# The sequence of a two-way GRU kept as channel, image, token, and one semaphore in place of two ahead of the candidate scan

## The chip, the cores and the metric

One Trainium2 chip, one of its cores. The metric is the device time of one launch in microseconds. A core has TensorE (matmuls; PE in the profile, PEld for its weight loads), VectorE (DVE), ScalarE (ACT), GpSimd (POOL) and SyncE (SP, whose queue issues the DMAs here). They run side by side and are ordered by semaphores: an instruction may wait until a counter has reached a value, and may raise a counter when it ends. SBUF and PSUM have 128 partitions; "a step" below is the distance between neighbouring elements of one partition.

## The reference

The input x is [16, 32, 32, 128] in f32: 16 images of 32 x 32 tokens of 128 channels.

```
xn   = layernorm(x) * gamma + beta                    # over the channels
gray = mean of xn over the channels                   # [16, 32, 32]
idx  = argmax of a small MLP on gradients of gray     # one choice per image
seq  = xn by rows, or by columns where idx == 1       # [16, 1024, 128]
z    = seq @ in_w.T + in_b
xp   = z @ wih.T + bih                                # per direction, 3 gates
for each of 1024 tokens (one direction forwards, one backwards), for all 16 images:
    gh = h @ whh.T + bhh
    r  = sigmoid(xr + hr);  u = sigmoid(xz + hz)
    n  = tanh(xn_ + r * hn)
    h  = (1 - u) * n + u * h
out  = x + concat(h forwards, h backwards) @ out_w.T + out_b
```

## The kernel before

**First stage, sixteen images.** An image is loaded to `xin` with 8 tokens per partition (image q in slot q mod 4). VectorE takes statistics (L728, L733), ScalarE the square root (`deviation`, L408), VectorE the reciprocal and the shift (`scales`, L740 and L743). ScalarE normalises 2 of the 8 tokens (L414), GpSimd the other 6 (L359). TensorE transposes the image into two PSUM banks, 4 x 128 columns each (L524). ScalarE then copies each bank twice, with gamma and beta (`evacuate`): to `seq` in the order of rows (L426) and to `seq_v`, a view of `big`, in the order of columns (L430); 512 columns per partition each time. VectorE sums the gray values (L754).

Per image, ScalarE's queue is in this order: normalise image q, first half of the writes of image q-1, square root of image q+1, second half of the writes of q-1. VectorE's is: statistics of q+1, gray sums of q-1, reciprocal and shift of q+1. TensorE folds in_w and wih into one weight (L537, L541) between the transposes of images 7 and 8.

**Scores.** After the last image the gray values go through some small matmuls (L552, L561, L565 and on) and some thirty VectorE instructions, one behind the other, to a mask of 16 images. ScalarE's square of the recurrent weights (L460) feeds a matmul (L557) that stands ahead of L561 in TensorE's queue. VectorE then copies `seq_v` over `seq` where the mask is set (`select`, copy_predicated, L856): the first and last 32 tokens at once, the other 960 in sixteen parts during the first sixteen rounds.

**Second stage, 1,024 rounds.** A round makes one step forwards (d = 0) and one backwards (d = 1). Both go through the same chain, half a round apart: TensorE multiplies the state, split in two f16 halves, with the recurrent weights for the reset gate, the candidate and the update gate, three matmuls of 16 columns each (`step`); ScalarE takes the reset gate's sigmoid (L488) and the update gate's (L491); VectorE makes the candidate's argument with a scan (`candidate`, L881); ScalarE takes tanh (L494); VectorE makes the new state (L892) and splits it (L901), and holds u * h ready (L908). Between the two steps of a round TensorE also does a part of the work for the block of 8 tokens that follows: a bias matmul, and one input product (`fill_input`, f32, two matmul instructions of 128 columns: 8 tokens x 16 images of `seq` as the moving operand), or an output projection (L872 adds it to x). All these matmuls are recorded at L590.

The candidate scan waits for two things, the reset gate from ScalarE and the recurrent product from TensorE:

```
dve.wait_ge(reset_ready[d], turn)
dve.wait_ge(hn_ready[d], turn)
```

An instruction carries one wait; of two in a row one becomes an instruction of its own (EVENT_SEMAPHORE, here at L880). TensorE's own order has two waits ahead of a step's reset group as well: the state's halves and `reset_ready` of the other direction.

The layouts: `seq` is [128, 1024 tokens, 16 images], the view `seq_v` the same. The same memory `big` later holds the tiles of x to which the output is added; the tiles of a block lie where tokens of `seq_v` lay that are already selected.

Of the kernel before, what the change touches and what calls it, by code (L numbers as in the profile page):

```python
# [20 lines left out]
P = 128  # L21
B, H, WD, C = 16, 32, 32, 128
L = H * WD
DI = 2 * C
HID = 128
TB = 8
# [74 lines left out]
def build(nc, x, gamma, beta, w1t, b1, w2t, b2, in_w, in_b, wiht, whht, bih, bhh, outwt, out_b, consts, out):  # L101
    ctx = ExitStack()

    def sb(name, shape, dt=F32):
        return ctx.enter_context(nc.sbuf_tensor(name, shape, dt))

    def sem(name):
        return ctx.enter_context(nc.semaphore(name))


    seq = sb("seq", [P, L, B])
    big = sb("big", [P, L * B])
    seq_v = big[:, :].rearrange("c (t b) -> c t b", b=B)
    tiles = big[:, :].rearrange("p (k c) -> p k c", c=C)
    xin = sb("xin", [P, SLOTS, TPP, C])
    stats = sb("stats", [P, SLOTS, TPP, 6])
# [104 lines left out]
    init_done = sem("init_done")  # L221

    reset_pre = [sem(f"reset_pre{d}") for d in range(2)]
    hn_ready = [sem(f"hn_ready{d}") for d in range(2)]
    update_pre = [sem(f"update_pre{d}") for d in range(2)]
    reset_ready = [sem(f"reset_ready{d}") for d in range(2)]
    update_ready = [sem(f"update_ready{d}") for d in range(2)]
    cand_pre = [sem(f"cand_pre{d}") for d in range(2)]
    state_ready = [sem(f"state_ready{d}") for d in range(2)]
# [11 lines left out]
    tile_in1 = sem("tile_in1")  # L241
    out_done = sem("out_done")
    tile_in = (tile_in0, tile_in1)

    x_tok = x.rearrange("b h w c -> b (h w) c")
    out_tok = out.rearrange("b h w c -> b (h w) c")
# [24 lines left out]
    @block.sync  # L271
    def _(sp):

        def load_image(rnd, q, wait):
            b = rnd * SLOTS + q
            if wait:
                sp.wait_ge(gray_sum, b + (1 - SLOTS))
                sp.wait_ge(xT_set, b * 2 + (2 - 2 * SLOTS))
            sp.dma_start(xin[:, q].rearrange("p j c -> p (j c)"),
                         x_part[bass.ds(b, 1)].rearrange("a p n -> (a p) n") if not isinstance(b, int) else x_part[b]  # L280
                         ).then_inc(x_in[q], 16)

        load_image(0, 0, False)
        load_image(0, 1, False)
        for dst, src in ((con[:, :], consts), (gb[:, 0:1], gamma), (gb[:, 1:2], beta),
                         (gamma_row[:, :], gamma.rearrange("c a -> a c").to_broadcast((P, C)))):
            sp.dma_start(dst, src).then_inc(first_in, 16)
        load_image(0, 2, False)
        load_image(0, 3, False)
        params = (  # L290
            (inw[:, :, :], in_w.rearrange("(k p) c -> p k c", p=P)),
            (inb[:, :], in_b),
            (wih[:, 0], wiht[0].rearrange("(k p) m -> p k m", p=P)),
            (wih[:, 1], wiht[1].rearrange("(k p) m -> p k m", p=P)),
            (whh[:, 0], whht[0]), (whh[:, 1], whht[1]),
            (outw[:, 0], outwt[0:HID]), (outw[:, 1], outwt[HID:2 * HID]),
            (mlp1[:, :], w1t), (mlpb1[:, :], b1), (mlp2[:, :], w2t),
            (mlpb2[:, :], b2.to_broadcast((B, 4))),
            (bih_col[:, :, :], bih), (bhh_col[:, :, :], bhh), (bias_col[:, 8:9], out_b),
        )  # L300
        assert len(params) == N_PARAM
        for q in range(SLOTS):
            load_image(1, q, True)
            for dst, src in params[q * 4:q * 4 + 4]:
                sp.dma_start(dst, src).then_inc(w_in, 16)
        with sp.Fori(2, B // SLOTS) as i:
            for q in range(SLOTS):
                load_image(i, q, True)


        sp.wait_ge(select_done, 1)

        def tile_rows(t, k):
            return t[:, k * TB:(k + 1) * TB, :].rearrange("b s c -> s b c")

        def load_tiles(k, q, wait):
            if wait is not None:
                sp.wait_ge(y_used, wait)
            for kk in (k, k * -1 + (NBLK - 1)):
                sp.dma_start(tiles[:, kk, :], tile_rows(x_tok, kk)).then_inc(tile_in[q], 16)  # L320

        load_tiles(0, 0, None)
        load_tiles(1, 1, None)
        sp.wait_ge(select_rest, 1)
        for i in range(1, NBLK // 4):
            for q in range(2):
                load_tiles(i * 2 + q, q, i * 4 + (2 * q - 2))

        for i in range(NBLK // 4, NBLK // 2):
            for q in range(2):  # L330
                for d in range(2):
                    k = i * 2 + q
                    kk = k if d == 0 else k * -1 + (NBLK - 1)
                    sp.wait_ge(y_used, i * 4 + (2 * q + d + 1))
                    sp.dma_start(tile_rows(out_tok, kk), tiles[:, kk, :]).then_inc(out_done, 16)
        sp.wait_ge(out_done, 16 * NBLK)

    N_INIT = 11
# [65 lines left out]
    def _(act):  # L404
# [15 lines left out]
        def evacuate(rnd, q, halves=(0, 1)):  # L420
            _, q1, turn = ahead(rnd, q, -1)
            for half in halves:
                act.wait_ge(xT_set, turn * 2 + (half - 1))
                src = bank[2 * (q1 % 2) + half]
                dst = seq[:, :, :].rearrange("c (p j) b -> c j p b", j=TPP)[:, 4 * half:4 * half + 4, :, bass.ds(turn - 1, 1)]
                act.activation(dst.rearrange("c j p b -> c j (p b)"), src[:, :].rearrange("c (j p) -> c j p", j=4),  # L426
                               ACT.Identity, bias=gb[:, 1:2], scale=gb[:, 0:1])
                dst = seq_v.rearrange("c (m j h) b -> c j h m b", m=WD // TPP, j=TPP)[
                    :, 4 * half:4 * half + 4, :, :, bass.ds(turn - 1, 1)].rearrange("c j h m b -> c j h (m b)")
                act.activation(dst, src[:, :].rearrange("c (j h m) -> c j h m", j=4, m=WD // TPP),  # L430
                               ACT.Identity, bias=gb[:, 1:2], scale=gb[:, 0:1]).then_inc(seq_set, 1)

        def image(rnd, q, first=False, last=False):
# [47 lines left out]
        def body(base, inverse, negative):  # L481
            for r in range(RING):
                q, s, e = r // TB, r % TB, r % 2
                turn = base + (r + 1)
                for d in range(2):
                    at = place(s, d) * COLS + d * B
                    act.wait_ge(reset_pre[d], turn)
                    act.activation(rpair[:, e, 2 * B * d:2 * B * (d + 1)].rearrange("p (n k) -> p n k", k=2)[:, :, 1],  # L488
                                   R[q][:, at:at + B], ACT.Sigmoid, scale=inverse).then_inc(reset_ready[d], 1)
                    act.wait_ge(update_pre[d], turn)  # L490
                    act.activation(thirds_of(gain, e, d)[:, :, 1],  # L491
                                   Z[q][:, at:at + B], ACT.Sigmoid, scale=negative).then_inc(update_ready[d], 1)
                    act.wait_ge(cand_pre[d], turn)
                    act.activation(thirds_of(drive, e, d)[:, :, 0],  # L494
                                   cand[:, (2 * e + d) * 2 * B:(2 * e + d + 1) * 2 * B].rearrange("p (n k) -> p n k", k=2)[:, :, 1],
                                   ACT.Tanh, scale=negative).then_inc(drive_ready[d], 1)
# [14 lines left out]
    def _(pe):  # L511
# [98 lines left out]
        def fill_input(q, kblk, g, d):  # L610

            kk = kblk if d == 0 else NBLK - 1 - kblk
            src = seq[:, kk * TB:(kk + 1) * TB, :]
            w = wcomb[:, d, g * HID:(g + 1) * HID]
            if g == G_N:
                return mm(nx(q)[:, :, d, :, 1], w, src)
            return mm(gate(R if g == G_R else Z, q)[:, :, d, :], w, src)
# [13 lines left out]
        def step(base, r, d):  # L631
# [14 lines left out]
            o, others = 1 - d, base + (r + d)  # L646
            alone = isinstance(base, int) and base + r + d == 0
            if not alone:
                pe.wait_ge(reset_ready[o], others)
            parts = ((0, high), (1, high), (2, low))  # L650
            run(G_R, parts).then_inc(reset_pre[d], 1)
            if not alone:
                pe.wait_ge(cand_pre[o], others)
            run(G_N, parts).then_inc(hn_ready[d], 1)
            if not alone:
                pe.wait_ge(update_ready[o], others)
            run(G_Z, parts).then_inc(update_pre[d], 1)
# [51 lines left out]
    def _(dve):  # L709
# [143 lines left out]

        def select(t0, t1):

            return v.copy_predicated(seq[:, t0:t1, :], mask[:, :].unsqueeze(1).to_broadcast([P, t1 - t0, B]),  # L856
                                     seq_v[:, t0:t1, :])


        select(0, EDGE)  # L860
# [5 lines left out]
        def add_output(j, d):  # L866

            dve.wait_ge(y_ready, j + 1)
            dve.wait_ge(tile_in[j % 2], min(32 * (j // 2 + 1), 8 * NBLK))
            kk = j if d == 0 else NBLK - 1 - j  # L870
            t = tiles[:, kk, :]
            v.tensor_tensor(t, Y[:, d * C:(d + 1) * C], t, ALU.add).then_inc(y_used, 1)  # L872


        def candidate(base, r, d):
            q, s, e = r // TB, r % TB, r % 2
            turn = base + (r + 1)
            at = (place(s, d) * 2 + d) * 2 * B
            dve.wait_ge(reset_ready[d], turn)
            dve.wait_ge(hn_ready[d], turn)  # L880
            v.tensor_tensor_scan(cand[:, (2 * e + d) * 2 * B:(2 * e + d + 1) * 2 * B],  # L881
                                 rpair[:, e, 2 * B * d:2 * B * (d + 1)], NX[q][:, at:at + 2 * B], 0.0,
                                 ALU.mult, ALU.add).then_inc(cand_pre[d], 1)
# [93 lines left out]
```

## Time and profile before

| | |
|---|---|
| time of three runs | 1751.23, 1752.12, 1759.0 us; median 1752.12 |
| profiled execution | 1756.46 us, of it 1754.6 span on the core |
| TensorE busy | 1626.4 us, 21,570 matmuls; weight loads 1286.7 us |
| VectorE busy | 1497.8 us, 9,055 instructions |
| ScalarE busy | 1204.6 us, 6,271 instructions |
| GpSimd busy | 57.3 us, 126 instructions |
| first selection | 114.4 us after the start |
| first recurrent step | 118.5 us after the start |

Busy counts leave out waits and other instructions of the sequencer. Matmuls are pipelined, so their recorded ends overlap the next ones' starts; from start to start is the better measure, for activations as well. Rows of the timeline give start, duration, engine, line, operation, output and inputs, shape and count; in square brackets the idle time before and what ended it.

### The profile page before, as it was taken

To read this page: it belongs to the slowest core of one execution; us is meant where nothing else is said; L and a number is where in the kernel's file an instruction comes from. 1 tells how busy PE (TensorE), PEld (TensorE's weight loads), DVE (VectorE), ACT (ScalarE), POOL (GpSimd) and SP (SyncE) were. 2 spreads that over 40 slices of the span, in tenths; PEclk is the share of its full clock that TensorE was granted. 3 is DMA by queue.
4 is the path that set the end of the run, shared out by engine and by line. 5 is a ranking of instruction groups with operands and counts; after the bars stand their busy time and mean duration, and the time that the engine had idled before them with its cause. 6 is when DMAs were issued, how large, how long until landed. Compare 5 with 4: busy or idle time off the path is not lost.

```text
span 1754.6 us, 63588 instructions
## 1 busy us (share of the span) xinstructions
PE 1626.4 (93%) x21570; PEld 1286.7 (73%) x21570; DVE 1497.8 (85%) x9055; ACT 1204.6 (69%) x6271; POOL 57.3 (3%) x126
## 2 busy tenths in 40 slices
PE   3548999999999999999999999999999999999997
PEld 2425777777777777777777777777777777777776
DVE  7879888888888888888888888888888888888887
ACT  7935666666666666666666666666666666666666
POOL 5520000000000000000000000000000000000000
PEclk9655555555555555555555555555555555555555
DMA  5200000000000000000000000000000000000000
GB/s 165 73 7 8 12 14 11 15 11 14 12 15 11 13 13 12 13 12 15 11 15 7 13 13 13 11 14 12 14 11 15 11 14 11 13 13 13 13 13 16
DMA packets 40118, 31.17 MB, mean 18 GB/s; under 512 B 3448, under 2 KB 37624, under 8 KB 39800
## 3 DMA queue, kind: packets, MB, share of 16 engines
q1 hardware_dynamic: 39800, 27.13, 5.3%
q8 instruction: 176, 2.88, 0.7%
q14 instruction: 142, 1.16, 0.2%
HBM read 18.73 MB, written 8.39 MB: 15 GB/s over the span
## 4 chain that ended last, share of the span: by engine, by line
PE 74%; DVE 11%; ACT 10%; issue 4%; DMA 0%; POOL 0%; SPq 0%; ACTq 0%; DVEq 0%; POOLq 0%
PE bank L590 73%; DVE bank L881 5%; ACT rpair L488 3%; ACT drive L494 3%; DVE state L892 3%; DVE halves L901 2%; ACT big L430 1%; ACT seq L426 1%; ACT xin L414 0%; DMA gamma_row<-in_gamma 0%; DVE seq L856 0%; PE bank L524 0%; POOL xin L359 0%; DVE drive L908 0%; PE bank L537 0%
## 5 line engine op out<-in xcount | busy, mean ns | idle before, releaser
L590 PEld LDWEIGHTS bank<-halves,wsplit 128*128 128x128 f16 x18432 | 730.2, 107 | 359.6 <-DVE halves L901 267.5
L590 PE MATMUL bank<-halves,wsplit 128*128 128x16 f16 x18432 | 917.4, 183 | 53.8 <-DVE halves L901 45.7
L892 DVE TENSOR_TENSOR_SCAN state<-gain,drive 128x48 f32<-128x48 f32 x2048 | 527.4, 258 | 180.3 <-ACT drive L494 6.1
L590 PE MATMUL bank<-seq,wcomb 128*128 128x128 f32 x1536 | 593.0, 491 | 0.2 <-DVE seq L856 0.2
L494 ACT ACTIVATE drive<-bank 128x16 f32<-128x16 f32 x2048 | 394.6, 193 | 237.3 <-DVE bank L881 34.5
L488 ACT ACTIVATE rpair<-bank 128x16 f32<-128x16 f32 x2048 | 378.1, 185 | 243.8 <-PE bank L590 243.8
L881 DVE TENSOR_TENSOR_SCAN bank<-rpair,bank 128x32 f32<-128x32 f32 x2048 | 462.4, 226 | 11.1 <-issue 7.7
L901 DVE SCALAR_TENSOR_TENSOR halves<-state 128x32 f16<-128x32 f32 x2048 | 399.1, 195 | 35.5
L491 ACT ACTIVATE gain<-bank 128x16 f32<-128x16 f32 x2048 | 392.9, 192 | 36.7
L590 PEld LDWEIGHTS bank<-seq,wcomb 128*128 128x128 f32 x1536 | 385.9, 312 | 0.7 <-DVE seq L856 0.7
L908 DVE SCALAR_TENSOR_TENSOR drive<-gain,state 128x16 f32<-128x16 f32 x2046 | 365.0, 178 | 1.6
L590 PE MATMUL bank<-ind,bias 6*128 6x128 bf16 (+1 forms) x768 | 297.9, 389 | 0.0
L590 PE MATMUL bank<-outw,state 128*128 128x128 f32 x512 | 197.9, 491 | 0.9 <-DVE state L892 0.9
L590 PEld LDWEIGHTS bank<-outw,state 128*128 128x128 f32 x512 | 128.7, 310 | 1.0 <-DVE state L892 1.0
L590 PEld LDWEIGHTS bank<-ind,bias 6*128 6x128 bf16 x768 | 75.5, 98 | 18.1
L524 PE MATMUL bank<-con,xin 128*128 128x128 f32 x128 | 29.7, 409 | 50.2 <-POOL xin L359 50.2
L872 DVE TENSOR_TENSOR big<-bank,big 128x128 f32<-128x128 f32 x256 | 72.3, 283 | 1.7 <-PE bank L590 1.3
L524 PEld LDWEIGHTS bank<-con,xin 128*128 128x128 f32 x128 | 23.8, 214 | 55.4 <-issue 35.0
L359 POOL TENSOR_SCALAR xin<-xin,rstd,shift 128x128 f32<-128x128 f32 x96 | 45.6, 495 | 36.9 <-DVE shift L743 28.6
L426 ACT ACTIVATE seq<-bank,gb 128x512 f32<-128x512 f32 (+1 forms) x32 | 41.8, 1307 | 0.0
L430 ACT ACTIVATE big<-bank,gb 128x512 f32<-128x512 f32 (+1 forms) x32 | 41.3, 1292 | 0.0
L590 PE MATMUL bank<-obias,ones 3*128 3x128 bf16 x128 | 36.2, 282 | 0.0
(114 smaller groups left out, 203.8 us busy)
## 6 DMA issues: line engine op xcount, KB each, us to landing
xin<-in_x SPq DMA_DIRECT2D x16, 512.0 KB, 3.6
big<-in_x SPq DMA_DIRECT2D x128, 64.0 KB
out<-big SPq DMA_DIRECT2D x128, 64.0 KB
wih<-in_wiht SPq DMA_DIRECT2D x2, 384.0 KB
con<-in_consts SPq DMA_DIRECT2D x1, 424.0 KB, 5.0
whh<-in_whht SPq DMA_DIRECT2D x2, 192.0 KB
inw<-in_in_w SPq DMA_DIRECT2D x1, 128.0 KB
outw<-in_outwt SPq DMA_DIRECT2D x2, 64.0 KB
```

Of the source, the lines that this page charges most:

```text
L426: act.activation(dst.rearrange("c j p b -> c j (p b)"), src[:, :].rearrange("c (j p) -> c j p", j=4), ACT.Identity, bias=gb[:, 1:2], scale ...
L430: act.activation(dst, src[:, :].rearrange("c (j h m) -> c j h m", j=4, m=WD // TPP), ACT.Identity, bias=gb[:, 1:2], scale=gb[:, 0:1]).then ...
L488: act.activation(rpair[:, e, 2 * B * d:2 * B * (d + 1)].rearrange("p (n k) -> p n k", k=2)[:, :, 1], R[q][:, at:at + B], ACT.Sigmoid, scal ...
L491: act.activation(thirds_of(gain, e, d)[:, :, 1], Z[q][:, at:at + B], ACT.Sigmoid, scale=negative).then_inc(update_ready[d], 1)
L494: act.activation(thirds_of(drive, e, d)[:, :, 0], cand[:, (2 * e + d) * 2 * B:(2 * e + d + 1) * 2 * B].rearrange("p (n k) -> p n k", k=2)[ ...
L524: ins = nc.tensor.transpose(bank[2 * (q % 2) + half][:, j * P:(j + 1) * P], xin[:, q, 4 * half + j, :], identity)
L590: return nc.tensor.matmul(o, w, m, start=start, stop=True, skip_group_check=True)
L872: v.tensor_tensor(t, Y[:, d * C:(d + 1) * C], t, ALU.add).then_inc(y_used, 1)
L881: v.tensor_tensor_scan(cand[:, (2 * e + d) * 2 * B:(2 * e + d + 1) * 2 * B], rpair[:, e, 2 * B * d:2 * B * (d + 1)], NX[q][:, at:at + 2 * ...
L892: v.tensor_tensor_scan(state[:, d, ring, :], gain[:, e, cols], drive[:, e, cols], 0.0, ALU.mult, ALU.subtract).then_inc(state_ready[d], 1)
L901: v.scalar_tensor_tensor(out=halves[:, e, d, :, :], in0=new[:, :, 2].unsqueeze(1).to_broadcast([P, 2, B]), scalar=-BIG, in1=both, op0=ALU. ...
L908: v.scalar_tensor_tensor(out=thirds_of(drive, e, d)[:, :, 1], in0=thirds_of(gain, e, d)[:, :, 1], scalar=-1.0, in1=old[:, :, 1], op0=ALU.a ...
```

## The change

`seq` becomes [128, 16 images, 1024 tokens] and `seq_v` likewise; the bytes and the counts of instructions that write, select and multiply are as before, in other orders of elements. The writes take their elements so that tokens lie side by side at the destination. Four residual tiles (`early`) go to `xin` slot 0 in place of `big`. The semaphores `hn_ready` and `reset_ready` become one, `reset_and_hn`, raised once by ScalarE and once by TensorE in each turn; the scan waits for two times its turn, and so does TensorE ahead of the other direction's reset group.

```diff
-    seq = sb("seq", [P, L, B])
+    seq = sb("seq", [P, B, L])
-    seq_v = big[:, :].rearrange("c (t b) -> c t b", b=B)
+    seq_v = big[:, :].rearrange("c (b t) -> c b t", b=B)
...
-    hn_ready = [sem(f"hn_ready{d}") for d in range(2)]
-    reset_ready = [sem(f"reset_ready{d}") for d in range(2)]
+    reset_and_hn = [sem(f"reset_and_hn{d}") for d in range(2)]
...
+    def tile_of(k):
+        early = (0, 1, NBLK - 2, NBLK - 1)
+        return xin[:, 0, early.index(k), :] if k in early else tiles[:, k, :]
...
-                dst = seq[:, :, :].rearrange("c (p j) b -> c j p b", j=TPP)[:, 4 * half:4 * half + 4, :, bass.ds(turn - 1, 1)]
-                act.activation(dst.rearrange("c j p b -> c j (p b)"), src[:, :].rearrange("c (j p) -> c j p", j=4),
+                dst = seq[:, bass.ds(turn - 1, 1), :].rearrange("c b (p j) -> c (b p) j", j=TPP)[:, :, 4 * half:4 * half + 4]
+                act.activation(dst, src[:, :].rearrange("c (j p) -> c p j", j=4),
                                ACT.Identity, bias=gb[:, 1:2], scale=gb[:, 0:1])
-                dst = seq_v.rearrange("c (m j h) b -> c j h m b", m=WD // TPP, j=TPP)[
-                    :, 4 * half:4 * half + 4, :, :, bass.ds(turn - 1, 1)].rearrange("c j h m b -> c j h (m b)")
-                act.activation(dst, src[:, :].rearrange("c (j h m) -> c j h m", j=4, m=WD // TPP),
+                dst = seq_v[:, bass.ds(turn - 1, 1), :].rearrange("c b (m j h) -> c j (b m) h", m=WD // TPP, j=TPP)[
+                    :, 4 * half:4 * half + 4]
+                act.activation(dst, src[:, :].rearrange("c (j h m) -> c j m h", j=4, m=WD // TPP),
                                ACT.Identity, bias=gb[:, 1:2], scale=gb[:, 0:1]).then_inc(seq_set, 1)
...
-                                   R[q][:, at:at + B], ACT.Sigmoid, scale=inverse).then_inc(reset_ready[d], 1)
+                                   R[q][:, at:at + B], ACT.Sigmoid, scale=inverse).then_inc(reset_and_hn[d], 1)
...
-            src = seq[:, kk * TB:(kk + 1) * TB, :]
+            src = seq[:, :, kk * TB:(kk + 1) * TB].rearrange("c b s -> c s b")
...
-                pe.wait_ge(reset_ready[o], others)
+                pe.wait_ge(reset_and_hn[o], 2 * others)
...
-            run(G_N, parts).then_inc(hn_ready[d], 1)
+            run(G_N, parts).then_inc(reset_and_hn[d], 1)
...
-            return v.copy_predicated(seq[:, t0:t1, :], mask[:, :].unsqueeze(1).to_broadcast([P, t1 - t0, B]),
-                                     seq_v[:, t0:t1, :])
+            return v.copy_predicated(seq[:, :, t0:t1], mask[:, :].unsqueeze(2).to_broadcast([P, B, t1 - t0]),
+                                     seq_v[:, :, t0:t1])
...
-            dve.wait_ge(reset_ready[d], turn)
-            dve.wait_ge(hn_ready[d], turn)
+            dve.wait_ge(reset_and_hn[d], 2 * turn)
```

## Rows read from the trace of the kernel before

**Rows 1.** Stretches: length, busy of PE, PEld, DVE, ACT, POOL; PEclk, DMA, GB/s.

```profile
60.00:80.00 20.00, 8.16 (x36) 6.58 (x35) 17.95 (x140) 20.00 (x30) 11.54 (x24) 0.50 0.25 79
...
600.00:900.00 300.00, 293.21 (x3971) 232.73 (x3970) 257.70 (x1568) 207.43 (x1140) 0.00 (x0) 0.50 0.05 13
```

**Rows 2.** Timeline of ScalarE in the first stage: two writes in a row.

```profile
20.92 1.26 ACT L426 ACTIVATE seq<-bank,gb 128x512 f32<-128x512 f32 x1
21.94 1.23 ACT L430 ACTIVATE big<-bank,gb 128x512 f32<-128x512 f32 x1
```

**Rows 3.** Timeline of VectorE: the shifts of images 3, 4 and 15.

```profile
21.95 0.17 DVE L743 SCALAR_TENSOR_TENSOR shift<-moments,rstd 128x8 f32<-128x8 f32 x1
...
26.38 0.17 DVE L743 SCALAR_TENSOR_TENSOR shift<-moments,rstd 128x8 f32<-128x8 f32 x1
...
80.53 0.17 DVE L743 SCALAR_TENSOR_TENSOR shift<-moments,rstd 128x8 f32<-128x8 f32 x1
```

**Rows 4.** Timeline of all engines, end of the first stage and first selection.

```profile
89.59 0.15 DVE L789 COPY xin<-xin 32x16 f32<-32x16 f32 x1
...
91.90 0.59 PE L557 MATMUL bank<-sums,con 128*128 128x1 f32 x2 [3.71 <-ACT square L460]
...
92.42 1.91 PE L561 MATMUL bank<-xin,con 32*32 32x512 f32 x2
...
114.42 1.34 DVE L856 COPY_PREDICATED seq<-mask,big 128x512 f32<-128x512 int32 x2
```

**Rows 5.** Timeline of VectorE and TensorE through one round.

```profile
801.28 0.23 DVE L881 TENSOR_TENSOR_SCAN bank<-rpair,bank 128x32 f32<-128x32 f32 x1
...
801.75 0.77 PE L590 MATMUL bank<-seq,wcomb 128*128 128x128 f32 x2
...
801.94 0.22 DVE L881 TENSOR_TENSOR_SCAN bank<-rpair,bank 128x32 f32<-128x32 f32 x1
...
802.32 0.43 PE L590 MATMUL bank<-halves,wsplit 128*128 128x16 f16 x9
...
802.85 0.23 DVE L881 TENSOR_TENSOR_SCAN bank<-rpair,bank 128x32 f32<-128x32 f32 x1
```

**Rows 6.** Timeline of TensorE near the end, forward steps of two rounds.

```profile
1741.45 0.41 PE L590 MATMUL bank<-halves,wsplit 128*128 128x16 f16 x9 [0.42 <-DVE halves L901]
...
1743.00 0.41 PE L590 MATMUL bank<-halves,wsplit 128*128 128x16 f16 x9 [0.42 <-DVE halves L901]
```

**Rows 7.** Timeline before the recurrence: an adjacent write and a stepped read.

```profile
95.42 1.05 ACT L466 ACTIVATE wcomb<-bank,sk 128x384 f32<-128x384 f32 x2 [2.72 <-DVE usual L802]
...
106.75 2.70 DVE L829 TENSOR_REDUCE pooled<-xin 32x48 f32<-32x1536 f32 x1
```

**Rows 8.** The page's groups: ScalarE in the rounds (busy us, mean ns; idle, releaser).

```profile
L494 ACT ACTIVATE drive<-bank 128x16 f32<-128x16 f32 x2048 | 394.6, 193 | 237.3 <-DVE bank L881 34.5
...
L491 ACT ACTIVATE gain<-bank 128x16 f32<-128x16 f32 x2048 | 392.9, 192 | 36.7
```

**Rows 9.** Timeline of TensorE: the transposes after the folding of weights.

```profile
52.50 1.07 PE L524 MATMUL bank<-con,xin 128*128 128x128 f32 x8
```

**Rows 10.** Timeline of TensorE: first input products and what follows.

```profile
115.82 2.93 PE L590 MATMUL bank<-seq,wcomb 128*128 128x128 f32 x12 [0.18 <-DVE seq L856]
118.54 0.43 PE L590 MATMUL bank<-halves,wsplit 128*128 128x16 f16 x9
118.90 0.39 PE L590 MATMUL bank<-ind,bias 6*128 6x256 bf16 x1
```

**Rows 11.** Timeline of TensorE: candidate's bias (half a bank) and input product.

```profile
812.08 0.39 PE L590 MATMUL bank<-ind,bias 6*128 6x128 bf16 x1
...
812.72 0.78 PE L590 MATMUL bank<-seq,wcomb 128*128 128x128 f32 x2
```

**Rows 12.** Line L880: count; duration ns minimum/median/maximum; first and last start.

```profile
L880 DVEq EVENT_SEMAPHORE  x2048: 21/21/131, 118.9 to 1748.7; - x187
```

**Rows 13.** Waits of VectorE: total us, times, longest us.

```profile
DVE bank L881 <- issue: 7.7, 31, 0.3
```

More of the change, by code:

```diff
@@ L319, in load_tiles @@
             for kk in (k, k * -1 + (NBLK - 1)):
-                sp.dma_start(tiles[:, kk, :], tile_rows(x_tok, kk)).then_inc(tile_in[q], 16)
+                sp.dma_start(tile_of(kk), tile_rows(x_tok, kk)).then_inc(tile_in[q], 16)
         load_tiles(0, 0, None)
@@ L334, in _ @@
                     sp.wait_ge(y_used, i * 4 + (2 * q + d + 1))
-                    sp.dma_start(tile_rows(out_tok, kk), tiles[:, kk, :]).then_inc(out_done, 16)
+                    sp.dma_start(tile_rows(out_tok, kk), tile_of(kk)).then_inc(out_done, 16)
         sp.wait_ge(out_done, 16 * NBLK)
@@ L870, in add_output @@
             kk = j if d == 0 else NBLK - 1 - j
-            t = tiles[:, kk, :]
+            t = tile_of(kk)
             v.tensor_tensor(t, Y[:, d * C:(d + 1) * C], t, ALU.add).then_inc(y_used, 1)
```

## The prediction

> **What bounds the kernel now.** I read the busy time by stretches first. The program has two stages that hardly overlap. Up to about 88 us sixteen images are normalised, transposed and written twice into the sequence buffers; in 60 to 80 us ScalarE is busy for all 20.00 us of 20 and VectorE for 17.95 [rows 1]. From 118 us on 1,024 rounds of the recurrence run, with TensorE at a granted clock of 0.50 (1.2 of 2.4 GHz); in 600 to 900 us ScalarE runs 1,140 activations, six to a round, so 190 rounds at 1.579 us [rows 1].
>
> In the first stage ScalarE sets the pace. A write to the sequence holds it for 21.94 - 20.92 = 1.02 us [rows 2]. VectorE's last step of an image, the shift, is 4.43 us after the one before while VectorE runs free (26.38 - 21.95); over images 4 to 15 it is (80.53 - 26.38) / 11 = 4.92 [rows 3]. Four writes are 4.08 of these 4.92; ScalarE's rest per image (normalising, square root) is 0.84, with no idle time, so the pace is ScalarE's. The stage ends late on ScalarE too: VectorE's gray rows are ready at 89.74, but TensorE's matmul on them (L561) starts at 92.42, because L557, ahead of it in TensorE's queue, waited until 91.90 for ScalarE's square of the weights, which stands behind the last write in ScalarE's queue [rows 4].
>
> In the second stage I went through one round in the timeline. It takes 802.85 - 801.28 = 1.57 us. TensorE has two recurrent steps in it and between them one input product with seq as the moving operand, in two f32 matmuls. That product starts at 801.75 and the next step at 802.32, with no idle time on TensorE [rows 5]. At the very end, where no input product is left, TensorE idles 0.42 us there and a round still takes 1743.00 - 1741.45 = 1.55 [rows 6]. So a chain through VectorE and ScalarE and the product on TensorE end within 0.02 us of each other: **the product has no slack left**, and whatever it grows by is paid in full.
>
> **The change part by part.**
>
> Writes to the sequence (32 + 32 activations of 512 columns). Before, each element lands 64 B or 512 B from the one before. After, seq is written in runs of four adjacent words and the transposed copy in runs of 32, and the price moves to the source, which is read from PSUM with a step of 512 B and 16 B. Where ScalarE writes adjacent words from PSUM (L466), two activations of 384 columns take 1.05 us, so 512 would take 1.05 x 512 / 768 = 0.70 [rows 7]. The other end is that the stepped PSUM read costs as much as the stepped write: 1.02 again, or above. The nearest rows of such a read: the tanh (L494) reads PSUM at every second word and takes 193 ns; the update gate (L491), with the same write and an adjacent read, takes 192 [rows 8]. One ns on 16 columns is next to nothing, so I take 0.70. ScalarE then needs 4 x 0.70 + 0.84 = 3.64 us per image, less than VectorE's 4.43, and VectorE sets the pace (this holds for any write up to (4.43 - 0.84) / 4 = 0.90). Gain over eleven images: 11 x (4.92 - 4.43) = 5.4 us. A part is lost: TensorE folds weights ahead of image 8's transposes, which start at 52.50 with no idle time before them [rows 9]; today ScalarE's backlog covers that. With the backlog gone the square root queued behind the late write comes late once; as an estimate I take one write, 0.7 us. So VectorE's part ends 4.7 us earlier. At the end of the stage ScalarE, no longer behind, has only the last image's writes left, so the square is done about when the gray rows are, and L561 follows these: 89.74 - 4.7 = 85.0 to 85.4 instead of 92.42 [rows 4]. All that is left before the recurrence hangs on VectorE's queue behind L561. Term: -7.0 us (-4.7 if the square stays last; 0 if the write stays at 1.02; about +18 at 1.3, where 16 images pay 4 x 0.28 each).
>
> Selection. The predicated copies keep their 960 elements (2 of 512), now in 16 runs of 60, and the mask is repeated inside a run. The two of 512 take 1.34 us together [rows 4], so one of 960 some 1.26, and sixteen of these stand in the first sixteen rounds. Runs of 60 adjacent words are like one run, and I find nothing that changes the price per element: 0; 10% either way would be 16 x 0.13 = 2 us.
>
> Input products. The moving operand was 128 adjacent words; now each word is 4,096 B from the one before. Twelve of these matmuls back to back take 2.93 us to the last modelled end, and the next matmul starts 118.54 - 115.82 = 2.72 after the first: about 0.22 us each, 1.7 ns a column [rows 10]. No row has a stepped moving operand. The nearest stepped read of SBUF is VectorE's reduction L829, one word in 64 B: 2.70 us for 1,536, so 1.76 ns a word with the instruction's fixed time in it [rows 7]. TensorE takes f32 columns hardly faster than that, so I take 0. Bounds: at the whole 1.76 ns, 0.06 x 128 = 8 ns a matmul, 1,528 matmuls, +12 us; if each matmul reads every word twice, in two sweeps, 2 x 128 x 1.76 = 0.45 us in place of 0.22, so +0.23 x 1,528 = +350 us. Below 0 there is nothing, since the read was adjacent before. One more pair speaks for 0: bias matmuls whose 128 results go to every second word of PSUM take 0.39 us, as much as those with 256 adjacent results [rows 10, 11]; the f32 input product of the candidate also writes every second word, and it takes 0.78 [rows 11], as one of the gates does, 0.77 [rows 5]. What halves the rate of narrow columns doesn't show in f32 ones.
>
> The Trainium skill, in "Advanced Engine Details and Errata", section "Memory Cachelines", says that SBUF wants at least two hits on a 16-byte line, else a read is penalised, and that any non-adjacent PSUM pattern slows matmuls. The bias pair agrees with its PSUM half, the f32 products don't; by its SBUF half the input products are the place that pays.
>
> Semaphores. VectorE has 2,048 separate wait instructions of 21 ns (L880), one ahead of each candidate scan [rows 12]; they go. The scan of direction 1 starts at 801.94 [rows 5]; behind it on VectorE stands the split of direction 0, which releases the step at 802.32. Freeing the scan by some 10 ns gains at most the 2 to 3 ns that TensorE's product leaves: -1.5 us over some 1,000 rounds. The mean round is 1.579 [rows 1], the one above 1.57: some 10 us over the stage. 7.7 of this is idle time ahead of the candidate scan that no wait explains ("issue", 31 times) [rows 13]. With 2,048 of VectorE's 11,100 instructions (9,055 busy ones and these) fewer to issue, I take 18% of it: -1.8 us; ends -7.7 (all gone) and +5 (estimates). The wait added on TensorE is that a reset group now also waits for TensorE's own candidate product of the other direction; three reset matmuls and the whole step are queued behind it. That product has been consumed by the scan at 801.94 when the step comes at 802.32 [rows 5], so 0.
>
> Residual tiles. The first four go into freed image buffers by the same transfers in the same order on the same queue, a dozen rounds before use: 0.
>
> **Sum.** -7.0 - 1.5 - 1.8 + 0 = -10.3. The profiled execution took 1756.46 us (span 1754.6), 4.3 above the median of 1752.12; its own time would become 1746.2, and set against the median I predict **1742 us**. About 0.5% (9 us) is what a measurement of this kernel tells from no change.
>
> **Rivals.**
> *The stepped moving read slows TensorE* (other side). Place: the two f32 matmuls between the steps of a round. For it: no slack [rows 5, 6]. Against it: 1.7 ns a column is already as slow as VectorE's stepped read. It decides from about 7 ns a matmul, where 1,528 x 7 = 11 us eats the gain. Mild form (10 to 25 ns): 1757 to 1780. Two sweeps: 1742 + 350 = about 2090. The Trainium skill's line rule above would give this rival.
> *The stepped PSUM read keeps the writes at 1.02 us.* For it: nothing in the trace reads PSUM at such steps over 512 columns. Then only the semaphore terms are left: 1752 - 4 = 1748; with 1.2 us a write, 1758 to 1762.
> *The semaphore does nothing*, and stalls only move to other instructions: 1752 - 7 = 1745.
>
> **How the numbers follow.** Forecast (front faster, product unchanged, semaphore terms anywhere in their bounds, the third rival within it) 0.55; PSUM read as dear as the write 0.17, dearer 0.03; product mildly slower 0.11; two sweeps or worse 0.14. The forecast's own range is 1735 to 1749. The range 1733 to 1772 leaves out the two sweeps (0.14) and the tails (0.05). Faster by over 0.5% (below 1743.4): two thirds of the forecast, 0.37. Within it: the forecast's rest, 0.18, the PSUM case, 0.17, and 0.02 of the others: 0.37. Slower: 0.26.
>
> **What would show it.** Writes at L426 and L430 with about 0.85 us in place of 1.3 and ScalarE idle in the first stage; shifts 4.4 to 4.5 us apart; the mask and the first selection near 107 instead of 114.4; no wait instructions at the candidate scan; input products of 421 to 560 ns as now and an undisturbed round of 1.565. It is wrong if the round is longer than 1.575, if the writes stay above 0.9 us from start to start, or if the first selection doesn't move.

## The result, and the profile after

| | before | after |
|---|---|---|
| median of five runs, us | 1751.76 (1751.23 to 1759.0) | 1731.27 (1730.61 to 1740.94) |
| ratio, 95% interval | 1 | 0.9888 [0.9858, 0.9917] |
| profiled execution, us | 1756.46, span 1754.6 | 1740.94, span 1739.1 |
| VectorE instructions, its sequencer's (separate waits above all) counted | 11,502 | 9,455 |

The change gains 20.5 us, twice the 10 forecast, and ends below the range. The profiled execution of after is the longest of its five (the other spans: 1728.8 to 1734.3), which matters for the first stage below.

Of the 15.5 us between the two spans, 1.1 lie ahead of the first candidate scan (119.12 to 118.03 us), 14.9 in rounds 16 to 1023 (1590.1 to 1575.2), and the sixteen rounds with selections and the tail are 0.2 longer each. Of the 14.9, 12.9 are the late rounds that the next part is about. So the term forecast as small (semaphores, -3.3 in all) is the large one, and in this execution the term forecast as large (first stage, -7.0) is nearly missing.

**The rounds.** The busy times of after by stretches, with the columns of [rows 1]:

```profile
60.00:80.00 20.00, 7.08 (x32) 5.57 (x32) 19.06 (x151) 17.87 (x33) 13.41 (x29) 0.59 0.29 97
...
600.00:900.00 300.00, 294.11 (x4008) 234.15 (x4007) 260.08 (x1584) 210.33 (x1151) 0.00 (x0) 0.50 0.05 13
```

In 300 us ScalarE now runs 1,151 activations, not 1,140: six to a round, 1.564 us a round, not 1.579. Yet one round looked at by itself is no shorter. VectorE's scans of direction 0 and TensorE's product with the step behind it, in the timeline of after:

```profile
801.68 0.23 DVE L884 TENSOR_TENSOR_SCAN bank<-rpair,bank 128x32 f32<-128x32 f32 x1
...
803.24 0.23 DVE L884 TENSOR_TENSOR_SCAN bank<-rpair,bank 128x32 f32<-128x32 f32 x1
```

```profile
802.14 0.78 PE L594 MATMUL bank<-seq,wcomb 128*128 128x128 f32 x2
802.73 0.42 PE L594 MATMUL bank<-halves,wsplit 128*128 128x16 f16 x9
```

1.56 us against 1.57 in [rows 5]; the median round is 1.567 before and 1.566 after. Before, the difference between mean and median is in a few rounds. Call a round late if it is over 0.03 us longer than the median: counted from the starts of the scans, before has 55 late rounds, 13.4 us in all, and after has 4, 0.5 us. The other 2.0 of the 14.9 us are in the undisturbed rounds: their mean is 1.5657 us before and 1.5638 here. But two more profiles of the same changed kernel have 1.5664 and 1.5633, so this part moves from execution to execution by as much as it differs here; why stays open. This is what a late round looks like in the timeline of before:

```profile
732.52 0.20 DVE L901 SCALAR_TENSOR_TENSOR halves<-state 128x32 f16<-128x32 f32 x1
732.95 0.23 DVE L881 TENSOR_TENSOR_SCAN bank<-rpair,bank 128x32 f32<-128x32 f32 x1 [0.23 <-issue]
```

The scan starts 0.43 us after the split ahead of it, 0.30 more than in other rounds, and nothing that it waits for explains it ("issue"). Numbered in VectorE's own order from 0, separate waits counted, the instruction that makes a round late, in every kernel run here, is number 125 in a block of 128. The queue that brings instructions shows blocks of this size: the page's rows of before, then of after:

```profile
q14 instruction: 142, 1.16, 0.2%
```

```profile
q14 instruction: 126, 1.03, 0.2%
```

16 packets and 0.13 MB fewer (8 KB each) for 2,047 instructions fewer: 128 to a packet. The Trainium skill ("Vector Engine (DVE) Microarchitecture Reference", section "Instruction fetch and dispatch (NX sequencer)") gives 64 bytes to an instruction; 128 of them are 8 KB, as the rows have it.

The page's row of the candidate scan in after has no "issue" left; its 7.7 us of 31 times in [rows 13] are gone (the 3.4 are the first scan of all):

```profile
L884 DVE TENSOR_TENSOR_SCAN bank<-rpair,bank 128x32 f32<-128x32 f32 x2048 | 459.3, 224 | 3.4 <-ACT rpair L492 3.4
```

**The first stage.** ScalarE's writes and VectorE's shifts (images 4 and 15) in after:

```profile
19.21 0.76 ACT L430 ACTIVATE seq<-bank,gb 128x512 f32<-128x512 f32 x1
19.87 0.76 ACT L434 ACTIVATE big<-bank,gb 128x512 f32<-128x512 f32 x1
```

```profile
27.06 0.17 DVE L747 SCALAR_TENSOR_TENSOR shift<-moments,rstd 128x8 f32<-128x8 f32 x1
...
82.02 0.17 DVE L747 SCALAR_TENSOR_TENSOR shift<-moments,rstd 128x8 f32<-128x8 f32 x1
```

A write takes 0.66 us from start to start (1.02 in [rows 2]), and ScalarE has over 2 us of every 20 to spare. But the last shift is later than in [rows 3], not earlier. TensorE, VectorE and ScalarE around the folding of weights, same kernel:

```profile
46.20 2.77 PE L541 MATMUL bank<-wih,inw 128*128 128x384 f32 x4
...
51.19 2.91 PE L541 MATMUL bank<-wih,inw 128*128 128x384 f32 x4
...
56.30 3.65 PE L528 MATMUL bank<-con,xin 128*128 128x128 f32 x16
57.53 0.78 ACT L430 ACTIVATE seq<-bank,gb 128x512 f32 x1 [5.47 <-PE bank L528]
59.19 0.20 DVE L744 RECIPROCAL rstd<-std 128x8 f32<-128x8 f32 x1 [3.95 <-ACT std L412]
```

The fold holds TensorE from 46.20 to 56.30, 10.1 us; before it ended at 52.50 [rows 9] after 6.6, because there its second half ran at nearly double rate:

```profile
45.87 2.77 PE L537 MATMUL bank<-wih,inw 128*128 128x384 f32 x4
49.87 1.54 PE L537 MATMUL bank<-wih,inw 128*128 128x384 f32 x4
```

During the longer fold no transposes come, ScalarE has nothing to write for 5.47 us, and VectorE then waits 3.95 for the square root behind these writes. What differs is TensorE's clock. The traces record each change of the granted clock: in before it rises to the upper level (2.4 GHz) at 48.80 us, in the fold, in after only at 60.37, behind it. (The view's 1.00 for stretches ahead of the first record is no measurement; more under "What was not expected".) The fold's length isn't a property of the change: of the other profiles here with the fold in one piece, one of the old layout (the semaphore alone) has the long fold as well, and all six of the new layout have the short one.

### The profile page after: what moved, and what is told of

It is laid out like the page before. It is cut to its first block, busy times and chain, and to the rows that moved or that the text cites. A ratio compares the mean times of both kernels' runs of the same rounds, so it can differ in the third digit from the quotient of the medians.

```text
span 1739.1 us, 61541 instructions
## 1 busy us (share of the span) xinstructions
PE 1622.2 (93%) x21570; PEld 1287.0 (74%) x21570; DVE 1496.9 (86%) x9055; ACT 1191.5 (69%) x6271; POOL 57.1 (3%) x126
## 4 chain that ended last, share of the span: by engine, by line
DVE 69%; ACT 21%; issue 8%; PE 1%; DMA 0%; POOL 0%; SPq 0%; DVEq 0%; ACTq 0%; POOLq 0%
DVE state L895 30%; ACT drive L498 21%; DVE bank L884 18%; DVE halves L904 12%; DVE big L876 4%; DVE seq L860 1%; DVE stats L732 1%; DVE weighted L758 1%; DMA gamma_row<-in_gamma 0%; DVE moments L737 0%; PE bank L541 0%; PE bank L545 0%; PE bank L594 0%; POOL xin L363 0%; PE bank L528 0%
## 5 line engine op out<-in xcount | busy, mean ns | idle before, releaser
L594 PE MATMUL bank<-halves,wsplit 128*128 128x16 f16 x18432 | 901.7, 182 | 47.6 <-DVE halves L904 44.6
L884 DVE TENSOR_TENSOR_SCAN bank<-rpair,bank 128x32 f32<-128x32 f32 x2048 | 459.3, 224 | 3.4 <-ACT rpair L492 3.4
L732 DVE BATCH_NORM_STATS2 stats<-xin 128x6 f32<-128x128 f32 x128 | 26.3, 278 | 7.1 <-DMA xin<-in_x 3.8
L758 DVE SCALAR_TENSOR_TENSOR weighted<-xin,gamma_row 128x128 f32<-128x128 f32 x128 | 29.9, 295 | 2.0 <-POOL xin L363 1.7
```

The source lines that it names most:

```text
L594: return nc.tensor.matmul(o, w, m, start=start, stop=True, skip_group_check=True)
L758: ins = v.scalar_tensor_tensor(out=weighted[:, j, :], in0=xin[:, q1, j, :], scalar=1.0, in1=gamma_row[:, :], op0=ALU.mult, op1=ALU.mult, a ...
```

## The experiments

**Each half of the change alone, a satisfied wait, and the changed kernel again** (one chip; before 1756.76 us, 1755.17 to 1760.23, ten runs). *Semaphore alone:* the kernel before with

```diff
-            dve.wait_ge(reset_ready[d], turn)
-            dve.wait_ge(hn_ready[d], turn)
+            dve.wait_ge(reset_and_hn[d], 2 * turn)
```

and what raises and reads `reset_and_hn`; old layout.

> The kernel before with the semaphores alone changed (layout as before). Theory A (the separate wait ahead of the candidate scan holds VectorE's sequencer until TensorE's product is there, so that where a late instruction block follows, every 128th instruction, its lateness can't be hidden): the late rounds, 55 before, fall to under 8, the undisturbed round to 1.565 or 1.566, the time to 1736 to 1739 us. Theory B, that of the prediction (late instructions only in proportion to VectorE's count of instructions, 18% fewer): some 45 late rounds, 1748 us. Theory C (the layout did it): 55 late rounds, 1750 to 1752 us.

Measured: 1745.06 us (1743.5 to 1745.93), ratio 0.9931 [0.9917, 0.9944], so -12.1 us; 4 late rounds, 0.5 us; mean round 1.563. That this comes so near to the 12.9 us of the late rounds is in part luck: the span of its profile is 12.3 shorter, of which the late rounds are -12.9, the undisturbed rounds -3.0 and a long fold (first scan at 122.75) +3.6. *Layout alone:* the changed kernel with the same lines turned back.

> The changed kernel with the two semaphores and two waits back, the layout as changed. Theory A: 50 to 60 late rounds as before, a round of 1.567, and only the gain of the first stage: 1744 to 1751 us, first selection 1 to 5 us earlier than before. Theory C (layout): few late rounds, 1735 to 1738 us. If the stepped moving read costs something at all, the undisturbed round is over 1.567.

Measured: 1750.93 us (1750.07 to 1753.72), 0.9966 [0.9954, 0.9979], -5.8 us; 55 late rounds, 13.4 us, as before; first candidate scan at 113.85 us, 5.3 earlier than before. The two halves, 0.9931 x 0.9966 = 0.9897, make up the whole (0.9894 below): they add, and the layout has no part in the rounds. Rounds by stretches, first of the semaphore alone (1,152 activations, 1.563 us), then of the layout alone (1,141, 1.578):

```profile
600.00:900.00 300.00, 294.08 (x4008) 234.11 (x4009) 260.03 (x1584) 210.41 (x1152) 0.00 (x0) 0.50 0.05 13
```

```profile
600.00:900.00 300.00, 292.99 (x3967) 232.35 (x3966) 258.04 (x1570) 208.18 (x1141) 0.00 (x0) 0.50 0.05 13
```

*A satisfied wait:* the changed kernel with a second wait ahead of each candidate scan, on a count that had been reached before the rounds began. There is a separate wait instruction again, and in the trace it is the satisfied one (L884); the scan carries the other.

```diff
             dve.wait_ge(reset_and_hn[d], 2 * turn)
+            dve.wait_ge(init_done, N_INIT)
```

> The changed kernel with a second wait put back ahead of each candidate scan, on a semaphore that has had its value since before the recurrence. VectorE issues as many instructions as before, but the separate wait is over at once. Theory A (it is the blocking that counts): late rounds stay under 10, 1730 to 1734 us, as the changed kernel. Theory B (the count): late rounds back to 50 or more, 1742 to 1745 us.

Measured: 1748.43 us (1742.79 to 1752.02), 0.9959 [0.9945, 0.9972]; 55 late rounds are back, 10.7 us. Its timeline at one of them, and its row of waits between 150 and 1720 us (us in total, times, longest):

```profile
724.01 0.20 DVE L905 SCALAR_TENSOR_TENSOR halves<-state 128x32 f16<-128x32 f32 x1
...
724.44 0.23 DVE L885 TENSOR_TENSOR_SCAN bank<-rpair,bank 128x32 f32<-128x32 f32 x1 [0.23 <-issue]
```

```profile
DVE bank L885 <- issue: 6.3, 31, 0.2
```

The profiled execution is the fastest of the five: its undisturbed rounds have a mean of 1.5605 us, the shortest of all profiles here. So Theory A falls: a wait that holds nobody up costs nearly as much as one that does (10.7 us of late rounds against 13.4; timed, 11.3 us above the changed kernel below, against 13.8 for the layout alone). Theory B has its 50 or more late rounds here, but as a share of the instructions it falls by the first run: with the semaphore alone the late rounds went from 55 to 4, not down by 18%.

> The changed kernel unaltered, for a second profile beside the first and the same chip's times. If the folding of weights takes 10 us as in the first profile, the first selection is at 113 us and the profiled execution near 1739 us; if its second half runs at twice the rate, as in the profile of before, the folding takes 6.6 us, the first selection is at 109 to 110 us. The rounds: under 8 late ones, undisturbed 1.566, in either case.

Measured: 1737.17 us (1736.85 to 1742.35), 0.9894 [0.9879, 0.9908]; 4 late rounds; first scan at 111.61.

**Kind of instruction, number, and place** (another chip; before 1755.16 us, 1754.61 to 1759.46, seven runs). The satisfied wait had brought back two things at once, a separate wait and 84 instructions in eight rounds in place of 68, with other instructions at the 128th places. *Two memsets:* the same 84, no waits.

```diff
                 if base + r > 0:
                     hold_state(base, r, 0)
+                v.memset(spare[0:1, 0:1], EPS)
...
                 if base + r > 0:
                     hold_state(base, r, 1)
+                v.memset(spare[0:1, 0:1], EPS)
```

> The changed kernel with two one-element memsets on VectorE in every round (one ahead of each new_state), so that VectorE again has 84 instructions per eight rounds, none of the added ones a wait. Theory A2 (a separate wait instruction on VectorE's queue, satisfied or not, keeps what stands behind it from being made ready early, so that the late instruction at every 128th place is felt only behind such waits): few late rounds, at most 8 of 1008 over 30 ns, as the 4 of the changed kernel; the time then differs from the changed kernel's only by what the memsets cost in the gaps of 0.07 to 0.14 us in which they stand (0 to 40 us, the same in every round). Rival B2 (the number of instructions, or where the 128th falls, is what counts): about 55 late rounds and 10 to 13 us, as with the satisfied extra wait, which has the same 84.

Measured: 1738.59 us (1737.16 to 1740.07), 0.9901 [0.9884, 0.9918]; 4 late rounds, 1.1 us. That is 4.3 us above the changed kernel beside it, 0.6 of it late rounds. In the profiles 1.0 more lies ahead of the first scan and 3.2 in undisturbed rounds (mean 1.5665 us); but the changed kernel in its second profile has 1.5664 without memsets, so that they cost anything is not shown. The packets are back at 142, so the blocks are; the stalls are not. Where the satisfied wait's scan at 724.44 was late, here the instruction of the same number (4733 on VectorE in both) is on time, 0.13 us behind its split:

```profile
722.95 0.20 DVE L905 SCALAR_TENSOR_TENSOR halves<-state 128x32 f16<-128x32 f32 x1
723.08 0.23 DVE L885 TENSOR_TENSOR_SCAN bank<-rpair,bank 128x32 f32<-128x32 f32 x1
```

The four that are left stand behind the separate wait that `add_output` still has:

```profile
DVE big L877 <- issue: 1.0, 4, 0.2
```

*One memset ahead of the rounds* (in front of the wait for `init_done`), which moves every 128th place on by one:

> The changed kernel with one memset on VectorE ahead of the rounds, once, so that every 128th place falls on another instruction of the round. Theory A2: a few late rounds (0 to 8) and the changed kernel's time within 0.3 %. Rival B3 (the changed kernel only happened to have its 128th places where a late instruction does no harm): tens of late rounds, 3 to 13 us slower than the changed kernel.

Measured: 1735.06 us (1734.79 to 1738.04), 0.9882 [0.9865, 0.9898]; 4 late rounds, 1.1 us, all four at `add_output` directly behind its wait. A2 holds against B2 and B3: it is neither the number nor the phase but the separate wait.

Counted over rounds 20 to 1015, what an instruction at the 128th place costs by how far behind a separate wait it stands. "Late by" is the time from the start of the VectorE instruction ahead (waits left out) to its own, against the median of the same place in other rounds (for a wait, the start of the instruction behind it):

| places behind the wait | kernel | times | late by, ns | round longer by, us |
|---|---|---|---|---|
| 1 (the scan of direction 0) | before | 15 | 300 to 321 | 0.30 to 0.32 |
| 1 (the scan of direction 1) | before | 16 | 344 to 362 | 0.34 to 0.36 |
| 1 (`add_output`) | one memset, two memsets | 4, 4 | 335, 313 | 0.28, 0.29 |
| 2 (new_state) | before, after | 4, 4 | 145 to 146 | 0.12 to 0.13 |
| 3 (hold; `add_output`'s wait) | before | 16, 4 | 178 to 198 | 0.13 to 0.16 |
| 3 (new_state of direction 0) | before | 11 | 0 | 0 |
| 3 (the scan of direction 1) | one memset | 4 | 5 to 22 | 0 to 0.02 |
| 5 (split) | before | 16 | 0 | 0 |
| 4 or more | two memsets | 78 | at most 5 | 0 |

Three places behind a wait, two kinds of instruction are late and two hardly or not. New_state starts 0.32 us behind the hold ahead of it in every round, since it waits for tanh, and that may cover a lateness; this was not tested.

**The fold in four pieces.** The changed kernel with the four parts of the fold behind the transposes of images 8 to 11:

```diff
+        for q in range(SLOTS):
+            transposes(2, q)
+            d = q // 2
+            if q % 2 == 0:
...
+            else:
...
-        with pe.Fori(2, B // SLOTS) as i:
-            for q in range(SLOTS):
-                transposes(i, q)
+        for q in range(SLOTS):
+            transposes(3, q)
```

> The changed kernel with TensorE's block of weight products (10.1 us in one piece in the profile of the changed kernel, where VectorE then waited 3.95 us; 6.6 us in the profiles with its second half at double rate) cut in four and put behind the transposes of four images. Theory F (the single block empties the pipeline of the first stage and took back what the faster writes had given): no wait of VectorE over 1 us for std between 40 and 90 us, first candidate scan at 108 to 112 us instead of 111.6 to 118.0, median 1 to 5 us below the changed kernel, spread of the runs smaller. Rival G (the pieces only move the same wait, or the busier TensorE is throttled earlier and the transposes slow down): first candidate scan at 112 to 118 us, no difference in the median. Rounds unchanged in both.

Measured: 1734.58 us (1733.82 to 1738.47), 0.9878 [0.9861, 0.9894], against 1734.33 for the changed kernel beside it: no gain. VectorE has no wait for the square root any more, as Theory F had it, but the first candidate scan comes at 112.93, a microsecond after that of the kernel beside it (111.92), which is no more than their loads explain (10.02 and 8.76, see below). With a short fold VectorE waits at most 0.2 us for the square root, so there is nothing to get, and six of seven profiles of the new layout have the short one. No version run here beats the changed kernel.

> The changed kernel once more, beside the others of this group. All theories: ratio to before 0.987 to 0.992, 4 late rounds; first candidate scan 111 to 114 us if the second half of the weight products runs at double rate, 117 to 119 us if not.

Measured: 1734.33 us (1734.03 to 1734.73), 0.9878 [0.9861, 0.9894]; 4 late rounds. Its fold's second half, the first transposes after it, the shifts of images 4 and 15, and the step that ends the stage:

```profile
48.01 1.54 PE L541 MATMUL bank<-wih,inw 128*128 128x384 f32 x4
...
50.64 1.07 PE L528 MATMUL bank<-con,xin 128*128 128x128 f32 x8
```

```profile
25.39 0.17 DVE L747 SCALAR_TENSOR_TENSOR shift<-moments,rstd 128x8 f32<-128x8 f32 x1
...
75.89 0.17 DVE L747 SCALAR_TENSOR_TENSOR shift<-moments,rstd 128x8 f32<-128x8 f32 x1
```

```profile
85.16 1.91 PE L565 MATMUL bank<-xin,con 32*32 32x512 f32 x2
```

L565 starts at 85.16 where its counterpart started at 92.42 [rows 4]; the first candidate scan is at 111.92, 7.2 us earlier than before. One more thing moves this number from run to run: when the load of `gamma_row` lands. The first statistics that wait for it, in before, after, and the changed kernel of this group:

```profile
9.72 1.65 DVE L728 BATCH_NORM_STATS2 stats<-xin 128x6 f32<-128x128 f32 x8 [2.19 <-DMA gamma_row<-in_gamma]
```

```profile
10.44 1.64 DVE L732 BATCH_NORM_STATS2 stats<-xin 128x6 f32<-128x128 f32 x8 [2.92 <-DMA gamma_row<-in_gamma]
```

```profile
8.76 1.65 DVE L732 BATCH_NORM_STATS2 stats<-xin 128x6 f32<-128x128 f32 x8 [1.07 <-DMA gamma_row<-in_gamma]
```

With this start taken out, the six profiles of the new layout with one short fold gain 5.6 to 7.4 us against before (119.12 at a start of 9.72): the layout alone 5.6 (113.85 at 10.05), the satisfied wait 6.4, the memsets 7.0 each, the changed kernel 7.4 and 6.2 (111.92 at 8.76). Between the two profiles with the long fold, the semaphore alone (122.75 at 9.46) and after (118.03 at 10.44), it is 5.7. The small front gain of the profiled execution, 1.1, is thus 5.7 less 3.9 for its long fold (the semaphore alone against before, both in the old layout) and 0.7 for its late load.

## Why the prediction was wrong

**First stage, -7.0: right.** Writes at 0.66 us (forecast 0.70, and the rival at 1.02 is out), VectorE sets the pace, L565 at 85.16, or 86.1 with its earlier load taken out (forecast 85.0 to 85.4). Timed alone -5.8 us [-3.7, -8.1]; by the profiles 5.6 to 7.4. Two details were off. The pace is (75.89 - 25.39) / 11 = 4.59 us an image, not 4.43, which both kernels reach only for some images, so the faster pace is worth 3.6 us and not 5.4. And the bubble at the fold, estimated at 0.7 us, is 0 to 0.2 with a short fold and 3.95 with the long one.

**Semaphores, the "issue" stalls, -1.8: the step that failed.** Measured: late rounds from 13.4 to 0.5 us, -12.9; the semaphore alone timed -12.1 us [-9.8, -14.6]. Two things were wrong. First, the rule: "With 2,048 of VectorE's 11,100 instructions (9,055 busy ones and these) fewer to issue, I take 18% of it: -1.8 us." The stalls don't go with the number of instructions, as the two memsets show (same number as before, 1.1 us). They go with the separate waits, and 2,047 of these were removed at once. Second, the size: the end "all gone" was put at the 7.7 us of VectorE's idle time in [rows 13]. That row counts VectorE's idle time ahead of one instruction, 0.25 us each time, but a round with it is 0.30 to 0.36 longer (10.0 us in all), and 24 of the 55 late rounds (3.3 us) have another late instruction, which is not in that row. The "some 10 us" between mean and undisturbed round stood in the same paragraph; it was nearer to the whole, and all of it went.

**Semaphores, the round, -1.5: not seen.** The median round is 1.567 us before and 1.565 to 1.567 in the three profiles of the changed kernel; over the stage the undisturbed rounds of these three come to -2.4 to +0.8 us against before, so 1.5 us can't be told from 0. The shortest undisturbed rounds of all, 1.5605, have the separate wait back, so it isn't the wait that this part moves with. The scan of direction 1 starts 0.175 us after new_state with the wait or without it, so the wait did not hold it.

**Input products, 0: right, for a reason that the prediction didn't have.** The stepped read isn't free: the first twelve products, up to the next matmul, take 117.46 - 114.67 = 2.79 us in after, 2.72 in [rows 10], 6 ns more for each (2.78 to 2.81 in all eight profiles of the new layout, 2.72 in both of the old).

```profile
114.67 2.96 PE L594 MATMUL bank<-seq,wcomb 128*128 128x128 f32 x12 [0.17 <-DVE seq L860]
117.46 0.41 PE L594 MATMUL bank<-halves,wsplit 128*128 128x16 f16 x9
```

In a round the next step's recorded start comes 0.586 us after the product's, not 0.570 (medians of 736 products): 8 ns a matmul, just what the prediction had set as the upper bound, and for which it had asked 12 us because "the product has no slack left". It had: the reset activation comes 0.878 us after the product's start in both, and the layout alone leaves the median round at 1.567. The recorded starts of a step's matmuls are not what the round turns on to 0.02 us. (The bound itself was rounded: 2.72 us over twelve matmuls of 128 columns are 1.77 ns a column, not 1.7, and so already the 1.76 of the reduction; and 1,524 of the matmuls, not 1,528, stand in the rounds.)

**Selection and residual tiles, 0: right.** A copy of 960 takes 1.23 us, 1.22 before (forecast 1.26), the sixteen rounds with them are 0.2 us longer in all, and VectorE has no wait of its own listed in the rounds of after.

**The rivals.** The semaphore does nothing: refuted, it is two thirds of the gain. The stepped moving read: 6 to 8 ns a matmul, about the 7 from which it was to decide, but not paid. The Trainium skill's line rule ("Advanced Engine Details and Errata", section "Memory Cachelines") has its sign right here; at 6 to 8 ns for 128 columns, hidden in the round, it moved no time that shows.

The sum with measured terms: -5.6 to -7.4 for the stage and -12.9 for the late rounds make -18.5 to -20.3; the medians say -20.5 [-14.5, -24.9].

## What to carry to other kernels

On a loop of short VectorE instructions, count the instructions that carry a second wait: each becomes a separate wait instruction, and merging two semaphores into one counted one removes it. When a mean round is longer than the median, list the late rounds and number the late instruction in its engine's own order before pricing the difference. Don't take one profile for the stage that isn't the steady loop: here its length moved by up to 6 us with a load's landing and with the rate of one block of matmuls. And take no granted clock from a stretch ahead of the first clock record: look at what the matmuls take.

## What was not expected of the hardware

- A satisfied wait of 21 ns costs nothing by itself (median round 1.560 us with it), but at one in 128 places the scan behind it starts 254 to 329 ns late, behind a wait that blocks 300 to 362, and an instruction four or more places behind a wait not at all. What is shown is the condition: the 128th place and a separate wait at most three places ahead. That the next block of instructions isn't read ahead past such a wait fits this and the packets of the instruction queue, but the reading itself is in no row. The Trainium skill ("Perfetto Trace Analysis", section "DVE / Act Engine Instruction") has an instruction's own wait moved to a queue while the sequencer goes on to the next one, which agrees with the 24 scans of after that stand at a 128th place with only their own wait and start on time to 10 ns; of a separate wait it gives no cost.
- TensorE's clock rises at a time that differs from execution to execution, and this sets the length of the fold. Its second four f32 matmuls of 384 columns took 1.54 us in seven profiles and 2.91 in two. By the traces' clock records the granted clock rises to 2.4 GHz at 45.8 to 49.0 us in the seven, during the fold and ahead of these matmuls, and at 59.6 and 60.4 in the two, behind the fold; by 63.8 us it is back at 0.50 in all nine. In before eight transposes of one image take 1.97 us ahead of the rise, 1.07 behind it [rows 9] and 1.97 again at 0.50 (from 59.04 on):

```profile
44.11 1.97 PE L524 MATMUL bank<-con,xin 128*128 128x128 f32 x8 [2.08 <-POOL xin L359]
...
59.39 1.97 PE L524 MATMUL bank<-con,xin 128*128 128x128 f32 x8 [3.96 <-POOL xin L359]
```

So TensorE ran at the lower level (1.2 GHz) ahead of the first record, though the view prints 1.00 there. Ahead of the rise it had been in the fold for 2.9 us in before and 14.2 in after, at like work; why it rose so late in the two stays open.
- ScalarE reads PSUM at steps of 512 B and 16 B as fast as adjacent words when it writes in runs of four or 32 words (0.66 us for 512; 0.70 as worked out from [rows 7]), while stepped writes took 1.02.
